# Conditioned mixing and a clamped low-rank linear layer: who issues the first mixer blocks, the order of the first loads, and the order of the passes of the down product

## The chip, the cores and the metric

One NeuronCore of a Trainium2 chip runs the kernel. The metric is the device time of one execution in microseconds; lower is better. Engines: TensorE (PE), VectorE (DVE), ScalarE (ACT), GpSimd (POOL) and SyncE (SP), which here only issues DMAs. TensorE's weight loads are shown apart (PEld), and the instructions that an engine's sequencer issues for DMAs carry a q (SPq, ACTq).

## The reference, cut to what matters

```python
# x [128, 64, 1024], condition [128], cond_w [16, 64, 64], W [1024, 1024], b [1024]
# A [8, 1024, 16], B [8, 16, 1024], p_scores [8]
y = einsum('bct,bcd->bdt', x, cond_w[condition])       # one 64x64 mixer for each sample
z = einsum('bsd,od->bso', y, W) + b
u = einsum('bsd,edr->ebsr', y, A)                      # the down product, 8 * 16 = 128 columns
m = einsum('ebsr,ero,e->bso', u, B, p_scores)          # the up product
gamma = minimum(0.5 * norm(z) / (norm(m) + 1e-6), 1.0) # norms over the last axis
out = x + z + gamma * m
```

Everything is float32.

## The kernel before

**Tiles.** Two samples of 64 channels make a tile of 128 rows by 1024; there are 64 tiles, worked in 32 pairs. The mixer of a tile is a 128 x 128 block-diagonal matrix of two 64 x 64 blocks, each fetched by a DMA whose address is read from the condition list (`value_load`, a register load, then `dma_start`). VectorE zeroes the mixer once; the blocks off the diagonal stay zero.

**Precision.** Products take fp32r operands. Each operand is split into a high part (ScalarE's cast, `*_hi`) and a low part (VectorE's subtraction of the high part, `*_lo`), and a product sums hi x hi, hi x lo and lo x hi. A 128 x 128 weight load goes before every matmul.

**TensorE's work for a pair** (`step` of the tensor block): the product of y with W is made of 512-wide quarters by a Strassen-like scheme of seven products (P1 to P7), twelve wide passes each (`product`, L899). T1 to T4 are sums of quarters of W, S1 to S4 sums of quarters of y. Beside them stand the mix of the next pair's tiles (`mix`, L886, plain fp32, sixteen short passes a tile), the down product and two up products (`up`, L950). The first pair (p = 0) is done ahead of the loop by eight plain products of the four quarters W11, W12, W21, W22 (`plain`), since T and S aren't there yet.

**The down product** (`down`, L932 to L941) sums 16 passes in one bank, u_ps of 512 columns. A wide pass multiplies a_hi of chunk k with y_hi and y_lo of both tiles side by side (512 columns, L938, the last one L940); a narrow one multiplies a_lo of chunk k with y_hi alone (256 columns, L939). They alternate over k, except that the last wide pass stands at the end. Ahead of it TensorE waits for y_hi and y_lo of the upper half of the pair's second tile (`y_ready(2 * p + 1, 1)`). ScalarE and VectorE then add the two halves and split u (`copy_u`, `sum_u`, `split_u`).

**Who waits on whom around it.** VectorE's order in the opening is written out by hand (L746 to about L810): y of tile 0 and W11's chunks in turn, y of tile 1, W12, W21, a_lo (L756), W22, then T3, the first biases, T1, T2, T4, y of tiles 2 and 3, S3 and S2, `bias_p1` (L744, releases P2 by p1_biased), z1 plus x (L795), gamma, and `add_m1` (L705, releases the up product by out1_ready). ScalarE follows the same order with the casts.

**Loads.** SyncE issues: the condition list, x of tile 0, then, after waits for the zeroed mixer and the list, the block mixer(0, 0), x of tile 1, mixer(1, 0), W11's chunks 2 and 3, W12, W21, a, W22, p_scores, B, bias, x of tiles 2 and 3. W comes in chunks of 256 KB. ScalarE issues W11's chunk 0, loads its activation table, waits as SyncE does, and issues mixer(0, 1), W11's chunk 1, mixer(1, 1). GpSimd issues no DMA. The two blocks of a tile count on one semaphore:

```python
pe.wait_ge(mixer_loaded[0], 16 * PER)        # PER = 2 blocks of a tile
```

Before the first mix TensorE runs eight matmuls on zeros to warm up (L972).

## Time and profile before

| what | value |
|---|---|
| median of 3 runs | 923.45 us (923.39 to 924.05) |
| the profiled execution, its own time | 922.94 us |
| its span, first to last instruction | 921.0 us |
| TensorE busy | 909.8 us, 99% |
| VectorE busy | 587.9 us, 64% |
| ScalarE busy | 367.5 us, 40% |
| GpSimd busy | 323.1 us, 35% |
| one trip of the loop for a pair | 28.2 us |

The profile is of one execution. The span leaves out what lies before the first and after the last instruction, 1.94 us. The times in the timeline are counted from the span's start. Matmuls are pipelined: the duration of a single one (0.39 us for 512 columns) is longer than the distance from one start to the next, and the distance is what a pass costs. A mix of four chunks is recorded as eight passes, two for each fp32 matmul.

### The profile page before, as it was taken

The page shows a single profiled execution, that of the slowest core. Times are in us where ns is not written, and L with a number is a line of the kernel's source. Part 1 is how long each engine was busy: PE and PEld are TensorE (multiplying, and loading weights), DVE is VectorE, ACT ScalarE, POOL GpSimd, SP SyncE. Part 2 cuts the span into 40 slices and gives each one's busy share as a digit, 9 for nine tenths or more (in the row PEclk, how much of TensorE's full clock was granted, in tenths as well). Part 3 has the DMA queues.
Part 4 walks back from the last instruction along what each step waited for, and adds up shares of the span by engine and source line. Part 5 has one row for each costly group of instructions (what it writes and reads, how often), then busy time and mean ns, then how long its engine had stood idle before and what let it go on. Part 6 is the DMA issues. An engine that isn't in the chain of part 4 may idle for free.

```text
span 921.0 us, 14732 instructions
## 1 busy us (share of the span) xinstructions
PE 909.8 (99%) x4628; PEld 772.7 (84%) x4628; DVE 587.9 (64%) x930; ACT 367.5 (40%) x727; POOL 323.1 (35%) x317
## 2 busy tenths in 40 slices
PE   8999999999999999999999999999999999999997
PEld 6888888888888888888888888888888888888885
DVE  5995766556665656665566656666655757566665
ACT  6653443334334333433343343334333433433342
POOL 0034443234433244432344322443323443224432
PEclk9999999999999999999999999999999999999999
DMA  8212221122221222211222212222112222122211
GB/s 288 86 70 95 76 90 65 51 94 94 71 93 42 76 94 71 94 57 59 94 94 71 93 35 83 94 71 94 49 68 94 94 71 84 37 90 94 73 47 68
DMA packets 32744, 75.16 MB, mean 82 GB/s; under 512 B 12761, under 2 KB 13786, under 8 KB 32730
## 3 DMA queue, kind: packets, MB, share of 16 engines
q1 hardware_dynamic: 32138, 74.17, 22.9%
q10 hardware_dynamic: 592, 0.82, 0.3%
q8 instruction: 7, 0.11, 0.1%
q14 instruction: 7, 0.06, 0.0%
HBM read 41.42 MB, written 33.55 MB: 81 GB/s over the span
## 4 chain that ended last, share of the span: by engine, by line
PE 94%; DVE 2%; DMA 1%; SPq 1%; issue 1%; ACT 0%; POOL 0%; DVEq 0%; POOLq 0%
PE b_ps L899 36%; PE c_ps L899 18%; PE mix_ps L886 12%; PE m_ps L950 9%; PE a_ps L899 9%; PE u_ps L938 6%; PE u_ps L939 3%; DMA a_lo_raw<-in_L_ffn_A_dram 1%; PE u_ps L940 1%; SPq L270 1%; DVE y L647 0%; DVE w_lo L602 0%; DVE w_lo_raw L614 0%; DVE w_lo L638 0%; DVE w_lo_raw L621 0%
## 5 line engine op out<-in xcount | busy, mean ns | idle before, releaser
L427 ACT CAST y<-mix_ps 128x512 fp32r<-128x512 f32 x126 | 74.5, 592 | 300.3 <-PE mix_ps L886 300.3
L368 POOL TENSOR_TENSOR stats<-stats 128x1 f32<-128x1 f32 x32 | 17.7, 553 | 459.8 <-ACT squares L480 459.8
L899 PE MATMUL b_ps<-w_hi,y 128*128 128x512 f32 x512 | 168.7, 390 | 0.0
L668 DVE TENSOR_TENSOR s_lo<-s,s_hi 128x512 fp32r<-128x512 f32 x124 | 134.4, 1103 | 4.2
L886 PEld LDWEIGHTS mix_ps<-mixer,x_in 128*128 128x128 f32 x1008 | 122.1, 192 | 6.0 <-DMA x_in<-in_x_dram 0.9
L886 PE MATMUL mix_ps<-mixer,x_in 128*128 128x128 f32 x1008 | 122.8, 275 | 0.1
L440 ACT CAST s_hi<-s 128x512 fp32r<-128x512 f32 x124 | 76.8, 620 | 114.1 <-POOL s L342 93.1
L354 POOL TENSOR_TENSOR z<-z,x_in 128x512 f32<-128x512 f32 x61 | 81.9, 1343 | 115.2 <-ACT squares L461 115.2
L647 DVE TENSOR_TENSOR y<-mix_ps,y 128x512 fp32r<-128x512 f32 x126 | 86.4, 687 | 45.8 <-ACT s L433 39.7
L899 PEld LDWEIGHTS b_ps<-w_hi,y 128*128 128x128 f32 x512 | 96.2, 188 | 19.2
L899 PE MATMUL b_ps<-w_lo,y 128*128 128x512 f32 x256 | 99.6, 389 | 0.0
L899 PE MATMUL c_ps<-w_hi,s_hi 128*128 128x512 f32 x248 | 99.1, 400 | 0.0
L899 PE MATMUL c_ps<-w_lo,s_hi 128*128 128x512 f32 x248 | 96.7, 390 | 0.0
L899 PE MATMUL c_ps<-w_hi,s_lo 128*128 128x512 f32 x248 | 96.6, 390 | 0.0
L899 PE MATMUL b_ps<-w_hi,s_hi 128*128 128x512 f32 x248 | 96.5, 389 | 0.0
L899 PE MATMUL b_ps<-w_lo,s_hi 128*128 128x512 f32 x248 | 96.5, 389 | 0.0
L899 PE MATMUL b_ps<-w_hi,s_lo 128*128 128x512 f32 x248 | 96.5, 389 | 0.0
L718 DVE TENSOR_TENSOR z<-b_ps,z 128x512 f32<-128x512 f32 x31 | 21.4, 692 | 106.0 <-PE b_ps L899 106.0
L899 PE MATMUL a_ps<-w_hi,y 128*128 128x512 f32 x264 | 86.6, 389 | 0.0
L938 PE MATMUL u_ps<-y,a_hi 128*128 128x512 f32 x224 | 80.4, 398 | 0.9 <-DVE y L647 0.9
L348 POOL TENSOR_TENSOR z<-z,x_in 128x1024 f32<-128x1024 f32 x30 | 72.0, 2401 | 0.0
L939 PE MATMUL u_ps<-y,a_lo 128*128 128x256 f32 x256 | 66.6, 281 | 0.0
(120 smaller groups left out, 1582.2 us busy)
## 6 DMA issues: line engine op xcount, KB each, us to landing
x_in<-in_x_dram SPq DMA_DIRECT2D x64, 512.0 KB, 3.6
out_dram<-z SPq DMA_DIRECT2D x62, 512.0 KB, 2.8
w_lo_raw<-in_L_ffn_W_dram SPq DMA_DIRECT2D x8, 256.0 KB, 6.7
mixer<-in_L_cond_weights_dram SPq DMA_DIRECT2D x126, 16.0 KB, 2.1
w_hi_raw<-in_L_ffn_W_dram SPq DMA_DIRECT2D x6, 256.0 KB, 7.0
out_dram<-z SPq DMA_DIRECT2D x3, 256.0 KB, 2.0
w_hi_raw<-in_L_ffn_W_dram ACTq DMA_DIRECT2D x2, 256.0 KB, 3.0
a_lo_raw<-in_L_ffn_A_dram SPq DMA_DIRECT2D x1, 512.0 KB, 8.2
```

Of the source, the lines that this page charges most:

```text
L348: nc.gpsimd.tensor_tensor(z1[:, :], z1[:, :], x_in[:, slot, :], ALU.add).then_inc(residual1_ready, 1)
L354: nc.gpsimd.tensor_tensor(z0[:, par, cols], z0[:, par, cols], x_in[:, 2 * par, cols], ALU.add).then_inc(residual0_ready, 1)
L427: nc.scalar.copy(y_part(y_hi, r, h), source(h)).then_inc(y_hi_ready, 1)
L440: nc.scalar.copy(s_hi[:, n, :, :], s_raw(n)).then_inc(s_hi_ready, 1)
L647: nc.vector.tensor_tensor(y_part(y_lo, r, h), source(h), y_part(y_hi, r, h).bitcast(fp32), ALU.subtract).then_inc(y_lo_ready, 1)
L668: nc.vector.tensor_tensor(s_lo[:, n, :, :], s_raw(n), s_hi[:, n, :, :].bitcast(fp32), ALU.subtract).then_inc(s_lo_ready, 1)
L718: nc.vector.tensor_tensor(z1[:, up_], b_ps[:, :], z0[:, par, up_], ALU.add).then_inc(u3_ready, 1)
L886: made = nc.tensor.matmul(source(h)[:, k, :], x_in[:, slot, (h * HC + k) * P:(h * HC + k + 1) * P], mixer[:, r, :], start=True, stop=True)
L899: summed = nc.tensor.matmul(bank, left[:, k, :], right[:, n, k, :], start=(start and k == 0 and i == 0), stop=(stop and k == HC - 1 and i ...
L938: nc.tensor.matmul(u_ps[:, :], a_hi[:, k, :], y[:, k, :, :], start=(k == 0), stop=False)
L939: nc.tensor.matmul(u_ps[:, 0:2 * P], a_lo[:, k, :], y[:, k, 0, :], start=False, stop=False)
L950: summed = nc.tensor.matmul(m[:, c], left[:, part], right[:, c], start=(n == 0), stop=(n == 2))
```

## The change

Four edits. (1) GpSimd issues the second block of both first mixers, mixer(0, 1) and mixer(1, 1), on semaphores of their own (`second_mixer_loaded`); ScalarE issues mixer(0, 0) and mixer(1, 0) and no longer W11's chunk 1; SyncE issues x of tile 1 right behind x of tile 0, then W11's chunks 1 to 3 and the rest of W, with no wait ahead of them. TensorE waits for both semaphores before the first two mixes, and later counts of `mixer_loaded` are one block lower (`mixer_count`). (2) ScalarE and VectorE split W11's chunk 0 ahead of the first half of y of tile 0, chunk 1 ahead of the second half. (3) W22 is loaded and split ahead of a. (4) The down product runs one wide pass, the eight narrow ones, and the other seven wide ones; the wait for y_lo of the second tile's upper half stands ahead of the wide pass of k = HC = 4, the others stay ahead of the product.

```diff
@@ -137,6 +137,7 @@
 
         x_loaded = [sem(f"x_loaded{s}") for s in range(4)]
         mixer_loaded = [sem(f"mixer_loaded{r}") for r in range(2)]
+        second_mixer_loaded = [sem(f"second_mixer_loaded{r}") for r in range(2)]
         out0_stored = sem("out0_stored")
         out1_stored = sem("out1_stored")
         w_loaded = {n: [sem(f"w{name}_{k}_loaded") for k in range(HC)]
@@ -213,6 +214,10 @@
             step(STEPS - 1, False, True)
 
 
+        def mixer_count(p):
+            return 16 * (PER * (p + 1) - 1)
+
+
         def halves(t, h):
             return 2 * t + h + 1
 
@@ -271,16 +276,12 @@
 
             sp.dma_start(cond_ids[:, :], condition.rearrange("(o n) -> o n", o=1)).then_inc(ids_loaded, 16)
             sp.dma_start(x_in[:, 0, :], x_tiles[0]).then_inc(x_loaded[0], 16)
-            sp.wait_ge(mixer_zeroed, 1)
-            sp.wait_ge(ids_loaded, 16)
-            sp.dma_start(first_mixer(0, 0), cond_block(first_condition(sp, 0, 0))).then_inc(mixer_loaded[0], 16)
             sp.dma_start(x_in[:, 1, :], x_tiles[1]).then_inc(x_loaded[1], 16)
-            sp.dma_start(first_mixer(1, 0), cond_block(first_condition(sp, 1, 0))).then_inc(mixer_loaded[1], 16)
-            load_w(W11, (2, 3))
+            load_w(W11, (1, 2, 3))
             load_w(W12)
             load_w(W21)
+            load_w(W22)
             sp.dma_start(a_raw, a.rearrange("(k p) e r -> p k (e r)", p=P)).then_inc(a_loaded, 16)
-            load_w(W22)
             sp.dma_start(p_col, p_scores.rearrange("(e o) -> e o", o=1).unsqueeze(1)
                          .to_broadcast([X, R, 1])).then_inc(p_loaded, 16)
             sp.dma_start(b_raw, bm.rearrange("e r o -> (e r) o")).then_inc(bm_loaded, 16)
@@ -375,6 +376,10 @@
             nc.gpsimd.memset(squares[:, :], 0.0).then_inc(idle_set, 1)
             nc.gpsimd.memset(half, 0.5).then_inc(half_set, 1)
             pool.wait_ge(half_set, 1)
+            pool.wait_ge(mixer_zeroed, 1)
+            pool.wait_ge(ids_loaded, 16)
+            for t in range(2):
+                pool.dma_start(first_mixer(t, 1), cond_block(first_condition(pool, t, 1))).then_inc(second_mixer_loaded[t], 16)
 
             def step(i, first, last):
                 for j in range(2):
@@ -503,20 +508,20 @@
             nc.scalar.activation(table_out, half, ACT.Square).then_inc(table_loaded, 1)
             act.wait_ge(mixer_zeroed, 1)
             act.wait_ge(ids_loaded, 16)
-            act.dma_start(first_mixer(0, 1), cond_block(first_condition(act, 0, 1))).then_inc(mixer_loaded[0], 16)
-            act.dma_start(raw11[:, 1, :], w_blocks[W11][1]).then_inc(w_loaded[W11][1], 16)
-            act.dma_start(first_mixer(1, 1), cond_block(first_condition(act, 1, 1))).then_inc(mixer_loaded[1], 16)
+            act.dma_start(first_mixer(0, 0), cond_block(first_condition(act, 0, 0))).then_inc(mixer_loaded[0], 16)
+            act.dma_start(first_mixer(1, 0), cond_block(first_condition(act, 1, 0))).then_inc(mixer_loaded[1], 16)
+            split_w(W11, (0,))
             split_y(0, 0, 0)
-            split_w(W11, (0,))
+            split_w(W11, (1,))
             split_y(0, 0, 1)
-            split_w(W11, (1, 2, 3))
+            split_w(W11, (2, 3))
             for h in range(2):
                 split_y(1, 1, h, mixed_1)
             split_w(W12)
             split_w(W21)
+            split_w(W22)
             act.wait_ge(a_loaded, 16)
             nc.scalar.copy(a_hi[:, :, :], a_raw).then_inc(a_hi_ready, 1)
-            split_w(W22)
             act.wait_ge(bm_loaded, 16)
             act.wait_ge(p_loaded, 16)
             nc.scalar.activation(b_raw, b_raw, ACT.Copy, scale=p_col).then_inc(bm_scaled, 1)
@@ -744,17 +749,18 @@
                 nc.vector.tensor_tensor(z0[:, par, up_], b_ps[:, :], bias[:, 1, :], ALU.add).then_inc(p1_biased, 1)
 
             nc.vector.memset(mixer[:, :, :], 0.0).then_inc(mixer_zeroed, 1)
+            split_w(W11, (0,))
             split_y(0, 0, 0, True)
-            split_w(W11, (0,))
+            split_w(W11, (1,))
             split_y(0, 0, 1, True)
-            split_w(W11, (1, 2, 3))
+            split_w(W11, (2, 3))
             for h in range(2):
                 split_y(0, 1, h, True, mixed_1)
             split_w(W12)
             split_w(W21)
+            split_w(W22)
             dve.wait_ge(a_hi_ready, 1)
             nc.vector.tensor_tensor(a_lo[:, :, :], a_raw, a_hi[:, :, :].bitcast(fp32), ALU.subtract).then_inc(a_lo_ready, 1)
-            split_w(W22)
             make_t3(0)
             make_t3(1)
             dve.wait_ge(bias_loaded, 16)
@@ -930,14 +936,22 @@
                 pe.wait_ge(u_hi_ready, p + 1)
                 pe.wait_ge(u_lo_ready, p + 1)
 
-            def down():
-
-
+            def down(p):
+
+
+
+                def both(k):
+
+                    return nc.tensor.matmul(u_ps[:, :], a_hi[:, k, :], y[:, k, :, :], start=(k == 0), stop=(k == KC - 1))
+
+                both(0)
                 for k in range(KC):
-                    if k < KC - 1:
-                        nc.tensor.matmul(u_ps[:, :], a_hi[:, k, :], y[:, k, :, :], start=(k == 0), stop=False)
                     nc.tensor.matmul(u_ps[:, 0:2 * P], a_lo[:, k, :], y[:, k, 0, :], start=False, stop=False)
-                summed = nc.tensor.matmul(u_ps[:, :], a_hi[:, KC - 1, :], y[:, KC - 1, :, :], start=False, stop=True)
+                for k in range(1, HC):
+                    both(k)
+                pe.wait_ge(y_lo_ready, halves(2 * p + 1, 1))
+                for k in range(HC, KC):
+                    summed = both(k)
                 summed.then_inc(u_done, 1)
 
             def up(r, m):
@@ -953,7 +967,7 @@
             def mix_next_0(i, j, p):
 
                 pe.wait_ge(x_loaded[2 * (1 - j)], 16 * (i + j + 1))
-                pe.wait_ge(mixer_loaded[0], 16 * PER * (p + 2))
+                pe.wait_ge(mixer_loaded[0], mixer_count(p + 1))
                 pe.wait_ge(s3_made, p)
                 mix(0, 2 * (1 - j), 0)
                 pe.wait_ge(s2_made, p)
@@ -962,7 +976,7 @@
             def mix_next_1(i, j, p):
 
                 pe.wait_ge(x_loaded[2 * (1 - j) + 1], 16 * (i + j + 1))
-                pe.wait_ge(mixer_loaded[1], 16 * PER * (p + 2))
+                pe.wait_ge(mixer_loaded[1], mixer_count(p + 1))
                 for h in range(2):
                     pe.wait_ge(y_lo_ready, halves(2 * p + 2, h))
                     mix(1, 2 * (1 - j) + 1, h)
@@ -971,11 +985,13 @@
             for _ in range(WARM):
                 nc.tensor.matmul(u_ps[:, :], idle[:, 0:P], idle, start=True, stop=True)
             pe.wait_ge(x_loaded[0], 16)
-            pe.wait_ge(mixer_loaded[0], 16 * PER)
+            pe.wait_ge(mixer_loaded[0], mixer_count(0))
+            pe.wait_ge(second_mixer_loaded[0], 16)
             for h in range(2):
                 mix(0, 0, h)
             pe.wait_ge(x_loaded[1], 16)
-            pe.wait_ge(mixer_loaded[1], 16 * PER)
+            pe.wait_ge(mixer_loaded[1], mixer_count(0))
+            pe.wait_ge(second_mixer_loaded[1], 16)
             for h in range(2):
                 mix(1, 1, h, mixed_1)
             for r, bank in ((0, b_ps[:, :]), (1, a_ps[:, :])):
@@ -988,10 +1004,11 @@
                 plain(bank, r, 1, W21)
             pe.wait_ge(a_hi_ready, 1)
             pe.wait_ge(a_lo_ready, 1)
-            down()
+            pe.wait_ge(y_lo_ready, halves(1, 0))
+            down(0)
             plain(c_ps[:, :], 0, 1, W22)
             pe.wait_ge(x_loaded[2], 16)
-            pe.wait_ge(mixer_loaded[0], 32 * PER)
+            pe.wait_ge(mixer_loaded[0], mixer_count(1))
             for h in range(2):
                 pe.wait_ge(y_lo_ready, halves(1, h))
                 mix(0, 2, h)
@@ -1017,8 +1034,9 @@
                         pe.wait_ge(u3_ready, p - 1)
                     product_y(b_ps, 0, 0, W11).then_inc(p_done[1], 1)
 
-                    y_ready(2 * p + 1, 1)
-                    down()
+                    pe.wait_ge(y_hi_ready, halves(2 * p + 1, 1))
+                    pe.wait_ge(y_lo_ready, halves(2 * p + 1, 0))
+                    down(p)
 
                     pe.wait_ge(p1_biased, p)
                     product_y(b_ps, 0, 1, W21, False).then_inc(p_done[2], 1)
```

## Rows read from the trace of the kernel before

**Rows 1.** The page: TensorE's share, and its weight loads (busy us, mean ns).

```profile
PE 909.8 (99%) x4628; PEld 772.7 (84%) x4628; DVE 587.9 (64%) x930; ACT 367.5 (40%) x727; POOL 323.1 (35%) x317
...
L899 PEld LDWEIGHTS b_ps<-w_hi,y 128*128 128x128 f32 x512 | 96.2, 188 | 19.2
```

**Rows 2.** Waits of TensorE, then VectorE, 0 to 45 us (total us, times, longest).

```profile
PE u_ps L938 <- DVE y L647: 0.9, 1, 0.9
PE m_ps L950 <- DVE z L782: 0.2, 1, 0.2
...
DVE a_lo L756 <- ACT a_hi L518: 1.5, 1, 1.5
DVE w_lo L602 <- ACT w_hi L411: 1.5, 1, 1.5
```

**Rows 3.** Timeline of the opening (start us, us, engine, line).

```profile
3.03 0.58 SPq L276 DMA_DIRECT2D mixer<-in_L_cond_weights_dram  x1
...
3.65 0.79 SPq L277 DMA_DIRECT2D x_in<-in_x_dram  x1
...
5.21 0.48 SPq L278 DMA_DIRECT2D mixer<-in_L_cond_weights_dram  x1
...
5.37 2.11 PE L886 MATMUL mix_ps<-mixer,x_in 128*128 128x128 f32 x16
...
9.00 2.02 PE L886 MATMUL m_ps<-mixer,x_in 128*128 128x128 f32 x16 [1.51 <-DMA mixer<-in_L_cond_weights_dram]
```

**Rows 4.** DMA issues in 2.9:3.6 and in 4.8:5.7 (KB, us to landing).

```profile
mixer<-in_L_cond_weights_dram SPq DMA_DIRECT2D x1, 16.0 KB, 2.2
...
mixer<-in_L_cond_weights_dram SPq DMA_DIRECT2D x1, 16.0 KB, 3.7
```

**Rows 5.** The chain that ended last, in order of time (start us, us).

```profile
47.69 2.74 PE b_ps L899 x12
...
51.79 2.72 PE a_ps L899 x12
...
57.23 1.78 PE mix_ps L886 x16
```

**Rows 6.** Busy time by stretch, last column GB/s; below, the chain's piece for a.

```profile
4.00:12.00 8.00, 6.43 (x41) 4.94 (x39) 3.27 (x6) 3.54 (x7) 0.00 (x0) 1.00 0.78 215
12.00:26.00 14.00, 14.00 (x63) 11.60 (x62) 12.47 (x18) 11.27 (x17) 0.00 (x0) 1.00 1.06 379
...
11.26 8.19 DMA a_lo_raw<-in_L_ffn_A_dram
```

**Rows 7.** Timeline of GpSimd, its first operations after the opening.

```profile
43.82 0.55 POOL L368 TENSOR_TENSOR stats<-stats 128x1 f32<-128x1 f32 x1 [42.12 <-ACT squares L480]
44.96 1.66 POOL L373 TENSOR_TENSOR stats<-stats 128x1 f32<-128x1 f32 x1 [0.58 <-ACT squares L489]
```

**Rows 8.** Timeline of VectorE in the opening.

```profile
7.86 0.68 DVE L602 TENSOR_TENSOR w_lo<-w_hi_raw,w_hi 128x512 fp32r<-128x512 f32 x1
...
46.11 0.70 DVE L744 TENSOR_TENSOR z<-b_ps,bias 128x512 f32<-128x512 f32 x1
...
48.56 1.28 DVE L705 SCALAR_TENSOR_TENSOR z<-m_ps,stats,z 128x1024 f32<-128x1024 f32 x1
```

**Rows 9.** Timeline of TensorE, one down product in the loop.

```profile
73.09 0.39 PE L938 MATMUL u_ps<-y,a_hi 128*128 128x512 f32 x1
73.32 0.28 PE L939 MATMUL u_ps<-y,a_lo 128*128 128x256 f32 x1
73.43 0.40 PE L938 MATMUL u_ps<-y,a_hi 128*128 128x512 f32 x1
...
75.44 0.40 PE L939 MATMUL u_ps<-y,a_lo 128*128 128x256 f32 x2
75.67 0.40 PE L940 MATMUL u_ps<-y,a_hi 128*128 128x512 f32 x1
75.90 0.40 PE L899 MATMUL b_ps<-w_hi,y 128*128 128x512 f32 x1
```

## The prediction

> **What bounds the kernel now.** I read the page first. TensorE is busy for 909.8 us of a span of 921.0 us [rows 1], so the other engines matter only where they hold TensorE up. A cheaper stream of passes on TensorE counts in every one of the 32 pairs of tiles; everything else counts once, in the opening. The waits of the first 45 us come next [rows 2, 3]: TensorE stands 1.5 us before the second mix, 0.2 us before the first up product and 0.9 us before the second down product. VectorE stands 1.5 us for a chunk of W11 and 1.5 us for a_hi. With the start and the tail of the kernel these make up the 11.2 us in which it is not busy.
>
> The timeline says why the second mix is late [rows 3]. SyncE issues its first mixer block at 3.03, x of tile 1 after that, its second mixer block at 5.21. The first mix runs from 5.37, the second from 9.00 though the first was over by about 7.3. The DMA view gives issue to landing [rows 4]: 2.2 us for SyncE's first block (landed 5.2, which is when the mix began), 3.7 us for the second (8.9, again the start of the mix). The first product follows 1.78 us later, at 10.78 (the length of a mix: 16 passes in 1.78 us [rows 5]).
>
> The queues are slack early and full later: 215 GB/s from 4 to 12 us, 379 GB/s from 12 to 26 us, and a lands at 11.26 + 8.19 = 19.45 [rows 6].
>
> **The opening, step by step.** SyncE loses two register loads and two mixer issues and gains one chunk of W11; x of tile 1 goes out at about 1.5 instead of 3.65, W from about 2.0 instead of 5.7. ScalarE loses that chunk's issue and keeps two mixer issues, so its second stands at about 4.3. GpSimd gets two register loads and two issues; it had nothing to do then, and does nothing until 43.8 [rows 7], so nothing is queued behind them. On SyncE's queue W11's chunk 1 now stands behind x of tile 1: landed by about 7.3, against 7.8 when ScalarE is through with the first y.
>
> What GpSimd pays for an issue no row shows. The nearest below is SyncE's 0.58 us for the same transfer [rows 3]; the nearest above is a small GpSimd operation of 1.66 us [rows 7]. I take 1.1, the middle. From the end of an issue to landing the two SyncE rows give 5.24 − 3.61 = 1.6 us and 8.9 − 5.7 = 3.2 us, the second with x of tile 1 in flight. Now x of tile 1 is in flight beside the first blocks too, with few bytes moved so far, so I take 2.0. GpSimd's first block then lands at 3.0 + 1.1 + 2.0 = 6.1 (ends: 5.2 as now, and 3.0 + 1.7 + 3.2 = 7.9). The first mix starts 0.7 us later than now, at 6.1. It takes 1.8, so the second wants to start at 7.9. GpSimd's second block, after 0.7 us of register load (4.44 to 5.21 between SyncE's issues), lands at 4.1 + 0.7 + 1.1 + 2.0 = 7.9 and ScalarE's at about 4.3 + 0.5 + 3.2 = 8.0; x, 0.5 MB directly behind x of tile 0, is there by 5.2 + 1.4 = 6.6 at 379 GB/s. The first product starts at about 9.65: **1.1 us earlier** (ends: 1.8 earlier with blocks as fast as now, 0.7 later with the slow end).
>
> The Trainium skill speaks against this part: "DMA: Bandwidth & Descriptors", section Specifications, gives a first byte after about 1 µs for a DMA issued from GpSimd and 0.6 µs for one from the other two. By that alone an estimate is 0.4 us of lateness and a gain of 1.4 in place of 1.1. [...]
>
> **VectorE's train.** Moving chunk 0 ahead of y takes 0.6 us out from behind the mix; x, W and a come early enough to close both idle times: 1.3 MB that the queues did not move before 12 us is 3.5 us at their full rate, so W22 ends near 16.5 and a near 18 though W22 goes first. W22 (four operations) covers a's landing on both engines; if a came after VectorE had finished W22 at about 20, that cover would be gone and down(0) still would not want it before 26. So VectorE is 1.5 + 1.5 + 0.6 − 0.7 = 2.9 us earlier when it starts on T3, and later is held back by TensorE alone (the last W22 product, some 1.1 earlier) to about 2.4.
>
> TensorE's stalls before the first up and the second down product are VectorE's lateness. For the down product, y_lo of tile 3's upper half came last; the new order asks for it only after one wide, eight narrow and three wide passes, 1.8 us later. What is late next is p1_biased (VectorE ends it at 46.81, TensorE wants it at about 47.6) and out1_ready (49.84 against 50.43, 1.36 before a_ps) [rows 5, 8]. With TensorE 1.1 + 0.2 + 0.9 + 0.1 = 2.3 earlier and 0.6 of room, VectorE must be 1.7 earlier; it is 2.4. So I count both stalls as gone: **1.1 us** (below: 0.3, if VectorE gains little).
>
> **The down product.** In the loop it runs from 73.09 to 75.90, 2.81 us [rows 9]. A pass in a product costs 2.72 / 12 = 0.227 us [rows 5]. The first pair costs 0.23 and 0.11; the six wide and five narrow passes between, 73.43 to 75.44, cost 2.01, where 6 × 0.227 + 5 × 0.113 is 1.93: about 0.235 and 0.12 each. Two narrow passes already stand together at 75.44 and with the change of width after them take 0.23, 0.115 each. The work is the same 16 passes; only the changes between widths fall from fourteen to two. With 8 × 0.227 + 8 × 0.115 it takes 2.74, 0.07 less; the product behind it, now 2.74 instead of 2.72, gives back part of 0.02. I take 0.08: **32 × 0.08 = 2.6 us**. Ends: 2.81 − 2.72 + 0.02 = 0.11, or 3.5 us; and with every wide at 0.235 and every narrow at 0.12, 2.84, that is 1.0 us lost. I stay near the upper end since both pure rows, twelve wide together and sixteen short mix passes at 1.78 / 16 = 0.111, run without the surcharge. In the loop the split wait costs nothing: y_lo is long there (no TensorE wait past 45 us). mixer_count changes constants alone.
>
> **Sum.** The profiled execution took 922.94 us around its span of 921.0, 0.5 below the median of the three runs, 923.45. 922.94 − 1.1 − 1.1 − 2.6 = 918.1, and against the median 918.6.
>
> **Rivals.**
> - *GpSimd's blocks come late.* A first use of that path, a slow issue and x in front: landing at 8 to 9, the first product no earlier or 1 to 2 us later than now. For it: the 3.7 us row. Against: even that row is for a queue in use. Gain 2.6 + 1.1 − 1.0 = 2.7: 920.7. Chance 0.17.
> - *The surcharge belongs to the mix of accumulations, not to their order.* Then the down product is worth under 0.02 us a pair, 0.6 in all: 923.45 − 2.8 = 920.7. For it: the surcharge outlasts the down product (47.69, 2.74 for 12). Against: two narrow passes at 0.115. Chance 0.12.
> - *VectorE still binds the opening*, because the queue to a is late or because p1_biased takes the place of y_lo: 0.9 comes back, 919.5. Chance 0.07.
> - *The other side: the narrow passes together show their weight loads.* A load is recorded at 188 ns [rows 1]; a wide pass of 227 hides it, a narrow one of 113 may not once eight follow each other. At 0.188 the run costs 7 × 0.075 = 0.53 more a pair, 17 us in all against 4.8: about 935. It decides from 7 × 32 × d = 4.8, d = 0.02, a narrow pass of 0.135. Against: mix passes, each with its load, at 0.111 for sixteen. Chance 0.03, with 0.01 for the code doing less than it says.
>
> **Numbers.** The forecast has 0.60. Range for 8 in 10: from 916.9 (1.8 + 1.1 + 3.5 = 6.4 is 917.1, and the run's spread) to 921.4, which takes in the first three rivals. A measurement of this kernel tells about 0.2%, 1.8 us: faster is under 921.6. Faster 0.60 + 0.13 + 0.09 + 0.06 = 0.88; same 0.08; slower 0.04.
>
> **What would show it.** TensorE's first mix near 6, the second directly behind it, the first product near 9.7; no wait before the first up or the second down product; VectorE without a gap from the first y until 26 us; a down product of 2.72 to 2.75 in the loop, from its first pass to the next product's. Wrong if the first mix starts past 8, if narrow passes stand over 0.12 apart, or if TensorE waits at the wide pass k = 4 or at the product after down.

## The result and the profile after

The changed kernel is slower, by 2.0 us: median 925.65 us of 15 runs (925.09 to 926.83), against 923.66 us (923.22 to 924.43) for 15 runs of the kernel before on the same chip. The ratio is 1.0022, 95% interval 1.0015 to 1.0028. The forecast was 918.6. The profiled execution took 925.39 us around a span of 923.8.

The page of the changed kernel answers to [rows 1]. TensorE is still busy 99% of the span, its busy time is 0.4 us longer, and its first mixes carry a wait that they did not have:

```profile
PE 910.2 (99%) x4628; PEld 774.1 (84%) x4628; DVE 588.6 (64%) x930; ACT 365.8 (40%) x727; POOL 321.8 (35%) x319
...
L892 PE MATMUL mix_ps<-mixer,x_in 128*128 128x128 f32 x1008 | 124.3, 277 | 4.3 <-DMA mixer<-in_L_cond_weights_dram 3.8
```

The timeline of the opening answers to [rows 3] (start us, duration, engine, line):

```profile
1.68 0.41 SPq L279 DMA_DIRECT2D x_in<-in_x_dram  x1
...
2.13 1.66 SPq L275 DMA_DIRECT2D w_hi_raw<-in_L_ffn_W_dram  x3
...
3.06 0.56 ACTq L511 DMA_DIRECT2D mixer<-in_L_cond_weights_dram  x1
...
3.70 0.69 POOL L382 DMA_DIRECT2D mixer<-in_L_cond_weights_dram  x1 [1.86 <-issue]
3.84 2.54 SPq L275 DMA_DIRECT2D w_lo_raw<-in_L_ffn_W_dram  x4
...
4.35 0.51 ACTq L512 DMA_DIRECT2D mixer<-in_L_cond_weights_dram  x1
...
4.90 0.52 POOL L382 DMA_DIRECT2D mixer<-in_L_cond_weights_dram  x1 [0.51 <-issue]
...
9.30 3.65 PE L892 MATMUL mix_ps<-mixer,x_in 128*128 128x128 f32 x16 [3.85 <-DMA mixer<-in_L_cond_weights_dram]
...
12.79 1.95 PE L892 MATMUL m_ps<-mixer,x_in 128*128 128x128 f32 x16
...
14.49 0.47 PE L905 MATMUL b_ps<-w_hi,y 128*128 128x512 f32 x1
```

SyncE issues x of tile 1 and W much earlier, as the change says, and the four blocks are issued by 5.4. But the first mix starts at 9.30, not 5.37 as before, and takes 3.65 us instead of 2.11. The second stands directly behind it. The first product starts at 14.49 against 10.78, 3.7 us later; the forecast had it 1.1 us earlier.

TensorE's waits up to 80 us, to be read against [rows 2]:

```profile
PE mix_ps L892 <- DMA mixer<-in_L_cond_weights_dram: 3.8, 1, 3.8
PE u_ps L986 <- POOL squares L376: 1.9, 1, 1.9
PE mix_ps L892 <- DVE y L652: 0.4, 1, 0.4
PE b_ps L905 <- DVE z L717: 0.3, 1, 0.3
```

The two waits before the first up and the second down product are gone, as forecast. Two smaller ones on VectorE are new: 0.4 us before a mix, 0.3 before a product. What made them is told below, behind the last runs.

The down product in the loop answers to [rows 9]. It is that of the pair p = 2, the same in both kernels. From the first pass to the next product it takes 79.68 − 76.89 = 2.79 us, where it took 2.81.

```profile
76.89 0.39 PE L945 MATMUL u_ps<-y,a_hi 128*128 128x512 f32 x1
77.12 1.11 PE L949 MATMUL u_ps<-y,a_lo 128*128 128x256 f32 x8
78.07 1.78 PE L945 MATMUL u_ps<-y,a_hi 128*128 128x512 f32 x7
79.68 0.39 PE L905 MATMUL b_ps<-w_hi,y 128*128 128x512 f32 x1
```

### The profile page after: what moved, and what is told of

Same layout as the page of the kernel before. It is cut to its first block, busy times and chain, and to the rows that moved or that the text cites. A ratio compares the mean times of both kernels' runs of the same rounds, so it can differ in the third digit from the quotient of the medians.

```text
span 923.8 us, 14733 instructions
## 1 busy us (share of the span) xinstructions
PE 910.2 (99%) x4628; PEld 774.1 (84%) x4628; DVE 588.6 (64%) x930; ACT 365.8 (40%) x727; POOL 321.8 (35%) x319
## 4 chain that ended last, share of the span: by engine, by line
PE 94%; DVE 3%; issue 1%; DMA 1%; ACT 0%; POOL 0%; POOLq 0%; DVEq 0%; ACTq 0%
PE b_ps L905 36%; PE c_ps L905 18%; PE mix_ps L892 12%; PE a_ps L905 9%; PE m_ps L964 9%; PE u_ps L945 6%; PE u_ps L949 3%; DVE w_lo L643 1%; DMA mixer<-in_L_cond_weights_dram 1%; DVE s_lo L673 0%; PE m_ps L905 0%; PE m_ps L892 0%; POOL stats L374 0%; DVE y L652 0%; DMA cond_ids<-in_itok_B_dram 0%
## 5 line engine op out<-in xcount | busy, mean ns | idle before, releaser
L355 POOL TENSOR_TENSOR z<-z,x_in 128x512 f32<-128x512 f32 x61 | 79.2, 1298 | 113.8 <-ACT squares L466 113.8
L945 PE MATMUL u_ps<-y,a_hi 128*128 128x512 f32 x256 | 69.3, 392 | 0.0
L905 PEld LDWEIGHTS a_ps<-w_hi,y 128*128 128x128 f32 x264 | 49.6, 188 | 10.3
```

Of the source, the lines that this page charges most:

```text
L355: nc.gpsimd.tensor_tensor(z0[:, par, cols], z0[:, par, cols], x_in[:, 2 * par, cols], ALU.add).then_inc(residual0_ready, 1)
L905: summed = nc.tensor.matmul(bank, left[:, k, :], right[:, n, k, :], start=(start and k == 0 and i == 0), stop=(stop and k == HC - 1 and i ...
L945: return nc.tensor.matmul(u_ps[:, :], a_hi[:, k, :], y[:, k, :, :], start=(k == 0), stop=(k == KC - 1))
```

## The experiments

A time with a ratio is the median of 10 or 11 executions; a time without one is of a single execution. The kernel before had a median of 923.6 or 923.7 us beside each. Its profiled execution took 922.94, 0.7 less than its median of 923.66, so two traces are compared by the times of their own executions.

**Which part costs.** down_only is the kernel before with the new down product alone; old_down is the changed kernel with the old one.

```diff
 # down_only: down(p) of the change, in before
-                    y_ready(2 * p + 1, 1)
-                    down()
+                    pe.wait_ge(y_hi_ready, halves(2 * p + 1, 1))
+                    pe.wait_ge(y_lo_ready, halves(2 * p + 1, 0))
+                    down(p)
```

> The kernel before with the new order of the down product alone (and its split wait). Theory: a down product with the passes standing together takes 2.793 us from its first pass to the next product instead of 2.813, and the product behind it loses its 0.02 us, so 0.04 us a pair and 1.2 us over 31 pairs; in the opening the wait of 0.9 us before the second down product turns into one of about 0.4 for p1_biased, worth another 0.4. About 1.6 us faster than before (ratio 0.9983), at least 1.2. Rival, that the new order itself costs in the loop and the changed kernel is slower for that: no faster, or slower than before.

> The changed kernel with the old order of the down product: loads, issuers and the order of the splits stay changed. Theory, that the loads alone make the changed kernel slower: 1.2 us slower than the changed kernel, so some 3.2 us above the kernel before (ratio 1.0035), first mix at about 9.3 as in the changed kernel. Rival, that the down product's order is at fault: at or below the time of before.

down_only took 922.02 us, ratio 0.9985 (0.9976 to 0.9994); old_down took 926.93, ratio 1.0033 (1.0024 to 1.0043). So the down product is a gain, of 1.3 us (old_down less the changed kernel) to 1.5 us, and everything else together is a loss of 3.4. The traces give its part in the loop more closely. These are the first passes of the down product of p = 31, first before, then in down_only, where that of p = 2 starts at 73.21:

```profile
890.70 0.39 PE L938 MATMUL u_ps<-y,a_hi 128*128 128x512 f32 x1
```

```profile
889.65 0.39 PE L939 MATMUL u_ps<-y,a_hi 128*128 128x512 f32 x1
```

Before, 29 trips of the loop take 890.70 − 73.09 = 817.61 us; in down_only they take 889.65 − 73.21 = 816.44. That is 0.040 us a trip. The old order gives 817.61 in splits_only too, and the new one 816.44 or 816.45 in warm22, x1_ahead, sp_holds, early_x1 and best.

Waits of TensorE in down_only:

```profile
PE mix_ps L886 <- DVE y L647: 0.5, 1, 0.5
PE b_ps L899 <- DVE z L712: 0.3, 1, 0.3
```

Neither of the two stalls of [rows 2] is left here. The larger one went by the split wait: VectorE ends y at 43.6, where the old order would have wanted it at 43.1 and the new one wants it at about 45. The smaller one did not. VectorE was already 0.8 us earlier than before ahead of the first down product, since chunks of W11 and a landed earlier in this execution (a_lo starts at 19.74 against 20.56). old_down, with the old order and TensorE 4.8 us later, has lost the smaller stall too and keeps 0.5 us of the larger one. And the gain of the opening is gone by the loop: TensorE is 1.5 us ahead at the second down product (43.09 against 44.62), and 0.1 us behind at that of p = 2 (73.21 against 73.09). Two other waits on VectorE, 0.8 us in all, and the restarts behind them took it back.

**Is it GpSimd's path?** In act_all ScalarE issues all four blocks and GpSimd none.

```diff
             act.dma_start(first_mixer(0, 0), cond_block(first_condition(act, 0, 0))).then_inc(mixer_loaded[0], 16)
+            act.dma_start(first_mixer(0, 1), cond_block(first_condition(act, 0, 1))).then_inc(second_mixer_loaded[0], 16)
             act.dma_start(first_mixer(1, 0), cond_block(first_condition(act, 1, 0))).then_inc(mixer_loaded[1], 16)
+            act.dma_start(first_mixer(1, 1), cond_block(first_condition(act, 1, 1))).then_inc(second_mixer_loaded[1], 16)
```

> The changed kernel with all four first mixer blocks issued by ScalarE and none by GpSimd; x and W still go out at once. Theory of the order of issue (a transfer's bytes move after all that was issued before it, whichever queue it stands in): the blocks land after the W chunks issued before them, the first tile's pair at about 9.0 and the second's at 10 to 11, first mix at 9 to 9.5, second directly behind. Rival, GpSimd's own path is what was late: the first pair lands at 5 to 6.5 and the first mix starts by 6.5.

926.22 us in one execution. First a piece of its chain of waits (start us, us), then its timeline:

```profile
4.23 5.35 DMA mixer<-in_L_cond_weights_dram
```

```profile
9.72 3.75 PE L890 MATMUL mix_ps<-mixer,x_in 128*128 128x128 f32 x16 [4.39 <-DMA mixer<-in_L_cond_weights_dram]
```

A block that ScalarE issues at 4.23 lands at 9.58, 5.35 us later, and the mix is as late as with GpSimd's. The queue that carries it is not the cause.

**Is it what was issued ahead?** In sp_holds the issuers are those of the change, but SyncE sends x of tile 1 and W only when the four blocks have landed.

```diff
             sp.dma_start(x_in[:, 0, :], x_tiles[0]).then_inc(x_loaded[0], 16)
+            for t in range(2):
+                sp.wait_ge(mixer_loaded[t], 16)
+                sp.wait_ge(second_mixer_loaded[t], 16)
             sp.dma_start(x_in[:, 1, :], x_tiles[1]).then_inc(x_loaded[1], 16)
```

> The changed kernel, but SyncE issues x of tile 1 and all of W only when the four mixer blocks have landed; ScalarE and GpSimd issue them as in the change. Theory of the order of issue: with only W's first chunk and x of tile 0 ahead, ScalarE's first block lands at about 5.1, GpSimd's at about 5.8 (0.7 us later issue), the second ones at 6.5 to 7; the first mix starts near 5.9, and x of tile 1, issued near 7, lands near 10. Rival, GpSimd's path is slow by itself: its first block still takes over 4 us from issue to landing and the first mix starts past 8.

The timeline of sp_holds:

```profile
3.72 0.69 POOL L385 DMA_DIRECT2D mixer<-in_L_cond_weights_dram  x1 [1.88 <-issue]
...
5.83 2.42 PE L895 MATMUL mix_ps<-mixer,x_in 128*128 128x128 f32 x16 [0.38 <-DMA mixer<-in_L_cond_weights_dram]
...
10.47 2.05 PE L895 MATMUL m_ps<-mixer,x_in 128*128 128x128 f32 x16 [2.22 <-DMA x_in<-in_x_dram]
```

The same GpSimd issue at 3.72 lets the mix start at 5.83. The total is no better (925.58 us in one execution), since x of tile 1 and W are now late (SyncE issues x of tile 1 at 6.95); that was the price of the test. The DMA view of the two kernels for the same stretch, 3.6 to 5.5 us, shows what moved. First the changed kernel (queues with packets and MB; issues with their KB and us to landing):

```profile
q1 hardware_dynamic: 168, 0.62, 86.5%
...
mixer<-in_L_cond_weights_dram ACTq DMA_DIRECT2D x2, 16.0 KB, 5.5
mixer<-in_L_cond_weights_dram POOLq DMA_DIRECT2D x2, 16.0 KB, 5.3
```

Then sp_holds:

```profile
q1 hardware_dynamic: 93, 0.32, 41.5%
q10 hardware_dynamic: 80, 0.02, 4.1%
q0 software_dynamic: 32, 0.02, 3.1%
...
mixer<-in_L_cond_weights_dram ACTq DMA_DIRECT2D x2, 16.0 KB, 2.2
mixer<-in_L_cond_weights_dram POOLq DMA_DIRECT2D x2, 16.0 KB, 2.0
```

q1 is SyncE's queue, q10 ScalarE's, q0 GpSimd's. In the changed kernel only SyncE's bytes move in this stretch, and the blocks' queues stand although both had been issued to; in the next stretch, up to 7.1 us, q1 is still the only queue with packets. In sp_holds all three move, in turn: up to 4.4 us q1 alone, with the rest of x of tile 0, from then the blocks' queues. A block waits for the big transfers that were issued before it, on whatever queue: 5.3 to 5.5 us from issue to landing, instead of 2.0 to 2.2. It does not wait for those issued after it: the chunk of W that SyncE issues at 3.84 in the changed kernel takes 6.4 us and lands at 10.2, behind the blocks of the first tile. Whether the block is held in the DMA engines or on its way to them, the traces do not tell.

The Trainium skill has two sentences on this. "DMA: Bandwidth & Descriptors", section Issuing engines are not separate DMA queues, says that transfers started by different engines share the same 16 DMA engines, and that a second issuer saves only sequencer time; the traces agree, with 5.3 us to landing for GpSimd's blocks in the changed kernel and 5.4 to 5.6 for ScalarE's in act_all. The section Queues, rings and completion order of the same page has each DMA engine take turns between its queues, packet by packet. That would have let a block pass the older bytes; in the stretch above no turn was given, and only from 7.1 us on do packets of all three queues move side by side.

**Why did the first mix take 3.65 us?** warm22 is the changed kernel with 22 dummy matmuls ahead of the first mix in place of 8.

```diff
-    WARM = 8
+    WARM = 22
```

> The changed kernel with 22 warm-up matmuls on zeros instead of 8, so that TensorE stands idle for about 1 us before the first mix instead of 3.85. Theory, that the first mix costs 3.65 us instead of 1.95 because the granted clock had fallen to the 1.2 GHz level in the idle time: the mix again starts at about 9.2 but takes about 1.8 to 2.0, the first product starts about 1.7 us earlier, at 12.8, and the execution is about 1.7 us shorter than that of the changed kernel (ratio to the kernel before about 1.0004). Rival, that the mix is slow because its operands or the queue are: still 3.6 us, no gain.

923.73 us, ratio 1.0001 (0.9992 to 1.0011), 1.9 us less than the changed kernel. Its timeline:

```profile
1.86 6.98 PE L986 MATMUL u_ps<-squares 128*128 128x512 bf16 x22 [1.86 <-POOL squares L376]
...
9.30 2.02 PE L892 MATMUL mix_ps<-mixer,x_in 128*128 128x128 f32 x16 [0.46 <-DMA mixer<-in_L_cond_weights_dram]
```

The block lands no earlier, and the mix is back at 2.02 us. The first product starts at 12.87 in place of 14.49. Busy time by stretch of warm22 (count of passes in brackets) shows the pace of the dummies, which are all alike:

```profile
2.00:4.00 2.00, 2.00 (x6) 0.64 (x5) 0.00 (x0) 0.79 (x2) 0.29 (x1) 1.00 0.91 305
...
6.00:8.00 2.00, 2.00 (x10) 0.88 (x9) 0.26 (x1) 0.00 (x0) 0.00 (x0) 1.00 1.03 360
```

Eight dummies take 3.59 or 3.60 us in every kernel but old_down, 14 more only 6.98 − 3.59 = 3.39: the pace doubles while they run. Here TensorE ran its first dummies at the lower of its two levels, 1.2 GHz, and went over to 2.4 GHz after it had been at work on them. Before, the first mix follows directly behind the dummies and takes 2.11 us. In the changed kernel TensorE stands 3.85 us after the dummies, and the whole mix goes at half pace, 3.65 us for sixteen passes. warm22 makes the warm-up longer and the stand shorter at once. old_down bears on the stand alone: its eight dummies took only 3.19 us, so they had already quickened, and behind a stand of 4.42 us its mix still took 3.75.

Eight dummies are hardly enough even without a long stand. In best, sp_holds, early_x1 and splits_only the stand before the first mix is 0.36, 0.38, 0.30 and 0.18 us, and the mix takes 2.18, 2.42, 2.48 and 2.65: some of its passes still go at half pace. The granted clock in the rows of the changed kernel has its first mix at the lower level too:

```profile
10.00:11.00 1.00, 1.00 (x7) 1.00 (x6) 0.00 (x0) 0.00 (x0) 0.00 (x0) 0.50 1.03 395
...
13.00:14.00 1.00, 1.00 (x11) 1.00 (x10) 0.68 (x2) 1.00 (x3) 0.00 (x0) 1.00 1.05 397
```

The column before the DMA share is that clock. It is not reliable to the microsecond: act_all has the same slow mix of 3.75 us with a granted clock of 1.00 throughout. The Trainium skill warns of that, in "TensorE: Matmul & The Clock Gate", section Seeing it yourself: single records of the clock are not to be trusted. The distances between passes are.

**How much comes from x of tile 1 alone?** x1_ahead has the issuers of before; the one change to who issues what, and in which order, up to 10 us is the line below. Splits, W22 ahead of a and the down product are the new ones.

```diff
             sp.dma_start(x_in[:, 0, :], x_tiles[0]).then_inc(x_loaded[0], 16)
+            sp.dma_start(x_in[:, 1, :], x_tiles[1]).then_inc(x_loaded[1], 16)
             sp.wait_ge(mixer_zeroed, 1)
             sp.wait_ge(ids_loaded, 16)
             sp.dma_start(first_mixer(0, 0), cond_block(first_condition(sp, 0, 0))).then_inc(mixer_loaded[0], 16)
-            sp.dma_start(x_in[:, 1, :], x_tiles[1]).then_inc(x_loaded[1], 16)
```

> The kernel before with the new order of the splits, W22 ahead of a and the new down product; of the issuing only x of tile 1 moved ahead of the first mixer blocks (SyncE: x of both tiles, then its two blocks, then W; ScalarE as before). Theory of the order of issue: the first blocks wait for x of tile 1 alone, land near 7.0, first mix at 7.0, second right behind at 8.8, first product at about 10.6. Rival, that each queue goes on by itself: ScalarE's first block lands at about 5.3, only SyncE's is late. Rival, that all was W's doing and x is harmless: first mix at 5.4.

923.62 us in one execution, against a median of 923.60 before. Its timeline:

```profile
7.33 3.72 PE L888 MATMUL mix_ps<-mixer,x_in 128*128 128x128 f32 x16 [2.02 <-DMA mixer<-in_L_cond_weights_dram]
```

Half a megabyte ahead of the blocks makes the mix 2.0 us later: 7.33 against 5.37. That was expected. That the mix would again take twice as long behind a stand of 2.0 us (3.72 us) was not; it took the gain that the early x should have given. The length of the stand alone does not do it: in sp_holds TensorE stands 2.22 us before its second mix, which takes 2.05. There the first mix had run at the upper level by its end; in x1_ahead the eight dummies had not left the lower one.

**What does a run of narrow passes cost?** narrow_twice is the changed kernel with the eight narrow passes done twice, so that a_lo counts twice in u.

```diff
-                for k in range(KC):
+                for k in [*range(KC), *range(KC)]:
                     nc.tensor.matmul(u_ps[:, 0:2 * P], a_lo[:, k, :], y[:, k, 0, :], start=False, stop=False)
```

> The changed kernel, its run of eight narrow passes done twice in a row (a_lo counted twice, so u is not the reference's). Theory, that a narrow pass with its weight load cannot go faster than 0.120 us for long: the sixteen narrow passes stand 0.113, 0.119, then 0.120 us apart throughout, and the wide passes behind them carry the same surcharge as behind eight (233, 235, 229, 232, 231 ns, 0.026 us in sum). Rival, a backlog that grows with the run: narrow passes go past 0.120 or the wide ones behind are surcharged longer.

955.54 us in one execution. A down product of its loop:

```profile
78.47 2.08 PE L949 MATMUL u_ps<-y,a_lo 128*128 128x256 f32 x16
80.38 1.78 PE L945 MATMUL u_ps<-y,a_hi 128*128 128x512 f32 x7
81.99 0.39 PE L905 MATMUL b_ps<-w_hi,y 128*128 128x512 f32 x1
```

Sixteen narrow passes take 80.38 − 78.47 = 1.91 us, eight took 78.07 − 77.12 = 0.95 in the changed kernel: 0.12 us each, however many. The seven wide ones behind take 1.61 us in both, 0.230 each, where a pure run of twelve costs 2.72 / 12 = 0.227 [rows 5]. So narrow passes in a run have a pace of 0.120, and grouping saves only on the changes between widths.

**The other parts alone.** splits_only is the kernel before with the new order of splits and W22 ahead of a. early_x1 has x of tile 1 directly behind SyncE's first block, as before, no chunk of W ahead of it on ScalarE's queue, and the other blocks on ScalarE's and GpSimd's. best keeps GpSimd out, has SyncE issue one chunk of W11 behind its two blocks, and moves T3 ahead of a_lo on VectorE. The last two have the new down product.

```diff
 # splits_only: loads, then ScalarE's and VectorE's splits
             load_w(W21)
-            sp.dma_start(a_raw, a.rearrange("(k p) e r -> p k (e r)", p=P)).then_inc(a_loaded, 16)
             load_w(W22)
+            sp.dma_start(a_raw, a.rearrange("(k p) e r -> p k (e r)", p=P)).then_inc(a_loaded, 16)
...
-            split_y(0, 0, 0)
             split_w(W11, (0,))
+            split_y(0, 0, 0)
+            split_w(W11, (1,))
             split_y(0, 0, 1)
-            split_w(W11, (1, 2, 3))
+            split_w(W11, (2, 3))
...
 # early_x1: SyncE and GpSimd, against the changed kernel
             sp.dma_start(x_in[:, 0, :], x_tiles[0]).then_inc(x_loaded[0], 16)
+            sp.wait_ge(mixer_zeroed, 1)
+            sp.wait_ge(ids_loaded, 16)
+            sp.dma_start(first_mixer(0, 0), cond_block(first_condition(sp, 0, 0))).then_inc(mixer_loaded[0], 16)
             sp.dma_start(x_in[:, 1, :], x_tiles[1]).then_inc(x_loaded[1], 16)
...
-            for t in range(2):
-                pool.dma_start(first_mixer(t, 1), cond_block(first_condition(pool, t, 1))).then_inc(second_mixer_loaded[t], 16)
+            pool.dma_start(first_mixer(1, 0), cond_block(first_condition(pool, 1, 0))).then_inc(second_mixer_loaded, 16)
 # best: SyncE as in early_x1, and behind x of tile 1
+            sp.dma_start(first_mixer(1, 0), cond_block(first_condition(sp, 1, 0))).then_inc(mixer_loaded[1], 16)
             load_w(W11, (1, 2, 3))
```

> The kernel before with the new order of the splits and W22 ahead of a alone; issuers, loads of the first mixers and the down product as before. Theory: the order by itself gives next to nothing, since VectorE waits for a's landing instead of W22's (a_lo is still the last operation ahead of T3 and ends about when all of W22 and a have landed): VectorE reaches T3 within 0.7 us of 24.1, TensorE's wait before the second down product stays between 0.3 and 1.5 us, the time is within 0.7 us of before (ratio 0.9993 to 1.0008). Rival, that W22 ahead of a was worth 1.1 us as predicted: ratio 0.9988 and no such wait.

> A version built on the order of issue: SyncE issues x of tile 0, mixer(0,0), x of tile 1, then all of W (W22 ahead of a); ScalarE W11's chunk 0, mixer(0,1), mixer(1,1); GpSimd mixer(1,0). Splits: W11's chunk 0, both halves of y of tile 0, W11's chunks 1 to 3, then as in the change; new down product. Theory: the first pair of blocks lands at 5.2 as before, x of tile 1 without W11's chunk 1 ahead of it at about 7.8 and the second pair with it, so the second mix starts near 7.9 and the first product near 9.7, 1.0 us earlier than in the kernel before; with 1.1 us of VectorE's stalls and 1.2 us of the down product about 3.3 us faster than the kernel before (ratio 0.9964). Rival, that VectorE or the loads of W take over: no better than the down product alone (0.9985).

> The kernel before with: the new down product; W11's chunk 1 issued by SyncE behind both its mixer blocks (so that x of tile 1 and the second blocks have one chunk less ahead of them); the splits in the order W11's chunk 0, both halves of y of tile 0, the rest as in the change; W22 ahead of a; and T3 made ahead of a_lo, so that VectorE does not wait for a. No DMA from GpSimd. Theory: second pair of blocks lands near 8.2 instead of 8.9, first product near 10.1 instead of 10.8, VectorE starts T3 about 1 us earlier than in the kernel before, and the waits before the first up and the second down product go: 0.7 + 0.8 + 1.2, about 2.7 us faster than before (ratio 0.9971). Rival, that the queues bind VectorE in another place (W11's last chunk, W22): no better than the down product alone, 0.9985.

splits_only took 924.0 us, ratio 1.0005 (0.9996 to 1.0014): nothing, and both stalls stay, at 0.8 and 0.3 us. early_x1 took 922.48, ratio 0.9989 (0.998 to 0.9998), a miss: it was to give 0.9964. best took 922.27, ratio 0.9986 (0.9977 to 0.9995), where 0.9971 was expected. Both have their first product earlier than before (10.24 and 10.00 against 10.78) and give it back. TensorE's waits in early_x1 behind the mixes:

```profile
PE b_ps L901 <- DVE w_lo L604: 0.6, 1, 0.6
PE mix_ps L888 <- DVE y L649: 0.5, 1, 0.5
PE b_ps L901 <- DVE z L714: 0.3, 1, 0.3
...
PE b_ps L901 <- DVE z L746: 0.3, 1, 0.3
```

best has the same four, with 0.4 on w_lo and 0.4 before the mix. The first of them is the loads' and not VectorE's. VectorE takes w_lo from ScalarE's w_hi, and that waited for a chunk of W11. The chain of waits in early_x1, then in best:

```profile
5.80 5.84 DMA w_hi_raw<-in_L_ffn_W_dram
```

```profile
5.74 4.09 DMA w_hi_raw<-in_L_ffn_W_dram
```

**What took the gains back.** VectorE has next to no idle time in this part of the kernel. Busy time from 26 to 64 us before (TensorE, its weight loads, VectorE, ...):

```profile
26.00:64.00 38.00, 36.94 (x194) 31.29 (x193) 37.65 (x52) 21.77 (x38) 9.73 (x6) 1.00 0.15 51
```

VectorE is at work for 37.65 of 38.00 us, so what makes one of its operations longer can reach TensorE. One operation does get longer. Before, around 55 us (GpSimd adds x to z, VectorE takes two halves of s_lo):

```profile
54.75 4.38 POOL L354 TENSOR_TENSOR z<-z,x_in 128x512 f32<-128x512 f32 x1 [6.41 <-ACT squares L461]
54.97 1.29 DVE L668 TENSOR_TENSOR s_lo<-s,s_hi 128x512 fp32r<-128x512 f32 x2
```

The same two in down_only:

```profile
53.93 1.45 POOL L354 TENSOR_TENSOR z<-z,x_in 128x512 f32<-128x512 f32 x1 [6.41 <-ACT squares L461]
54.14 2.39 DVE L668 TENSOR_TENSOR s_lo<-s,s_hi 128x512 fp32r<-128x512 f32 x2
```

The two engines do not run these side by side at full pace. Before and in splits_only GpSimd's addition takes 4.38 us and VectorE's two subtractions 1.29. In all ten other traces the addition takes 1.44 or 1.45 us and the subtractions 2.38 or 2.39, so VectorE is 1.1 us later from there on. These ten are also the traces with a wait of 0.4 or 0.5 us before a mix at this place; before and splits_only have none. In down_only it undoes VectorE's lead of 0.8 us, and with it what the two stalls had given. That the two operations hold each other up is read from their durations; which of them gives way, and why it was the other one before, no run was made to settle. It is not the down product: old_down has the old one and is among the ten. No opening that was tried beats down_only beyond the intervals.

**The sum, from rows alone.** The down product of p = 2 is a good mark, since everything of the opening and of this collision lies ahead of it. From there on the new down product gives 30 times 0.04, 1.2 us. Each trace is held against the time of its own execution, less the 922.94 of before's; the last column has the differences of the medians.

```
kernel       down p=2  against before  loop   sum    own time  medians
before       73.09      0               0      0      0         0
after        76.89     +3.8            -1.2   +2.6   +2.5      +2.0
down_only    73.21     +0.1            -1.2   -1.1   -1.1      -1.5
old_down     77.95     +4.9             0     +4.9   +4.7      +3.4
act_all      77.60     +4.5            -1.2   +3.3   +3.3
sp_holds     76.47     +3.4            -1.2   +2.2   +2.6
warm22       75.22     +2.1            -1.2   +0.9   +0.8      +0.1
x1_ahead     74.95     +1.9            -1.2   +0.7   +0.7
early_x1     74.07     +1.0            -1.2   -0.2   -0.4      -1.1
splits_only  73.58     +0.5             0     +0.5   +0.5      +0.3
best         73.56     +0.5            -1.2   -0.7   -0.7      -1.5
```

The sums hold within 0.2 us of the own times, save for sp_holds, which lost 0.5 us more behind the loop; its cause is open. The medians lie 0.2 to 1.3 us lower against before, for the most part because its profiled execution was a quick one. In the changed kernel the first product is 3.7 us late and the down product of p = 2 is 3.8 us late: the stalls that went gave nothing. In old_down half of the second mix went at half pace too, and its first product starts at 15.55.

## Why the prediction was wrong

**The opening, forecast 1.1 us earlier, was 3.7 later.** This is the step that failed, and in it one sentence: that x of tile 1 would be in flight beside the first blocks "with few bytes moved so far, so I take 2.0" from the end of an issue to landing. What counts is not what has moved but what has been issued. By 3.8 us SyncE and ScalarE had sent off x of both tiles and W11, x 1 MB and W 1 MB, and the blocks stood behind most of it: 5.3 to 5.5 us from issue to landing. The row that should have set the term was in hand: 3.7 us for SyncE's second block [rows 4], with x of tile 1 and a chunk of W11 issued shortly ahead of it. It was read as the slow end for one block, when the change puts every block behind more than that. GpSimd's own cost, on which most of the working went, was small: 0.69 and 0.52 us for an issue, where 1.1 was taken, and 2.0 us to landing in sp_holds, no slower than ScalarE's 2.2 there and SyncE's 2.2 before. The later first byte for GpSimd that the Trainium skill gives ("DMA: Bandwidth & Descriptors", section Specifications) shows in no landing of these runs. A slip of 0.1 us stands in the sum as well: the second mix was put at 7.9, though the block of its own that it needs was put at 8.0.

**The clock was not priced at all.** The mix was costed at 1.78 us wherever it stood. Behind eight dummies it had the full pace only in before and down_only, where it followed at once. warm22 puts the price at 1.9 us by the medians and 1.7 by the traces, nearly the whole net loss. The rival "GpSimd's blocks come late" named the right place and a landing "at 8 to 9", but the wrong cause, and without the clock its 920.7 was 5 us short.

**The down product, forecast 2.6 us, gave 1.2.** The sign was right and the size off. The term took narrow passes at 0.115, between what two of them cost [rows 9] and the pure mix passes; they hold 0.120 in a run, and the wide ones behind a run are still a little over 0.227. The saving is 0.040 us a pair, not 0.08, as the 29 trips show. The rival in which the surcharge belongs to the mix of accumulations gave under 0.02, so the truth lay between it and the forecast. The other-side rival, weight loads showing at 188 ns, is out: sixteen narrow passes in a row keep 0.120. Why 0.120 and not 0.113 was not found.

**The stalls, forecast 1.1 us, went and gave nothing.** VectorE's earlier train was to close them. splits_only has that order, with the old issuers, and keeps them; down_only has the old one and loses them. The larger went by the split wait, which asks for y_lo's upper half 1.8 us later; the smaller went with a VectorE that was 0.8 us earlier in down_only, or a TensorE that was later in the other kernels. The prediction had named p1_biased and out1_ready as next, and counted 0.6 us of room. What came next was something that it had not named: VectorE's two subtractions at 54 to 59 us take 1.1 us longer beside GpSimd's addition, and TensorE then waits before a product and a mix. The rival "VectorE still binds the opening" had the right engine, though neither of its two reasons. In down_only 1.5 us of lead turned into 0.1 us of lag between 43 and 73 us. That VectorE had no slack there was to be read in the trace of before, 37.65 of 38.00 us; a mean of 64% for the whole span hid it. That the operation would get longer was not to be read there, except that GpSimd's addition took 4.38 us, against a median of 1.30.

## What to carry to other kernels

Before moving a small, urgent transfer to another engine's queue, add up the bytes issued ahead of it on all queues: they are what it waits for, and the issuing engine hardly matters. Price a delay of TensorE's first real work with the clock: if the warm-up ends long before the work begins, the work runs at half pace. When a stall is removed in an opening where two engines run neck and neck, follow the gain to the first mark behind it, here a down product of the loop: a shorter wait at one place says nothing of what is left of it. On the way, compare the durations of the same operations in both traces, for one that got longer can take the whole gain. And hold a trace against the time of its own execution, not against a median.

## What the hardware did that was not expected

- Blocks issued on ScalarE's and GpSimd's queues at 3.06 and 3.70 moved no packet up to 7.1 us while SyncE's queue had older work; with at most the rest of x of tile 0 ahead (sp_holds) they landed in 2.0 to 2.2 us.
- GpSimd's addition of x and VectorE's subtractions at 54 to 59 us held each other up: 4.38 us for the addition and 1.29 for the subtractions in two traces, 1.45 and 2.39 in ten.
- A stand of 2.0 us between dummies and mix (x1_ahead) left the mix at half pace throughout, 3.72 us; with the mix directly behind them (before) it took 2.11. Behind a mix that had reached the upper level, 1.5 us (before) and 2.2 us (sp_holds) of standing did no harm: the second mix took 2.02 and 2.05.
- The granted clock in the records did not always follow the passes: 1.00 in act_all and in x1_ahead beside mixes at half pace.
- GpSimd's issue of an address-register DMA costs 0.69 us, then 0.52, against SyncE's 0.58 and 0.48.
- Passes of 256 columns in a run hold 0.120 us, those of 512 columns 0.227: more than half.
